# A stack of sequence layers on one core: attention inputs with a swap product, and mixing levels written out with the output scaled once

## The chip, the cores and the metric

The kernel runs on one core of a Trainium2 chip. The metric is the device time of one execution in microseconds (us). Each stage of the kernel ends with a barrier of all engines, so the stages don't overlap. Engines are named as in the profile: PE (matmul; PEld is its weight load), DVE (vector), ACT (scalar), POOL (GpSimd), SP (its queue issues DMAs).

## The reference, cut to what matters

`x` is 2 x 2048 x 256, float32. Eight layers each add their result to `x`: a recurrence, a slot layer, the mixing layer, a slot layer, a long convolution, a ternary layer, attention, a ternary layer. The change touches the mixing layer (`_L0_attn_b`) and the attention (`_L1_attn_b`).

```python
q, v = (qv[..., :c], qv[..., c:])          # qv = x @ attn_W + attn_b
n = 1
while n < t:                                # t = 2048: 11 levels
    prev = concatenate([broadcast(identity, (b, n, c)), q[:, :t - n]], axis=1)
    f = concatenate([prev, q], -1) @ freq_W + freq_b
    z = concatenate([sin(f), cos(f)], -1) @ out_W + out_b
    q = z / (max(abs(z), axis=-1) + 1e-6)
    n *= 2
return (q * v) @ proj_W + proj_b
...
q, k, v = proj(Wq), proj(Wk), proj(Wv)      # 16 heads of 16
re, ro = te * cos - to * sin, te * sin + to * cos    # te, to: even and odd entries of q and of k
```

## The kernel before

**Mixing levels** (`mix_levels_phase`). Between levels the kernel keeps, instead of `q`, the two frequency products of `q` (`parts`, 128 x 2048 for each of two batches). A level has 8 units (`NG`) of 512 tokens (`GT`), 11 levels have 88, in four blocks of 128 tokens (`GP`). For each unit PE sums the two parts, one of them shifted by the level's distance, into `p_f` (`freqs`, L1404 and L1405, four passes). ACT adds the bias (`g`, L1437). DVE takes it into one turn in four operations (L1486 `turns`, L1488 `off`, L1490 and L1492 `red`). POOL clamps it (`arg`, L1472). ACT takes the sine (`sc`, L1441). PE multiplies by the output weights (`products`, L1413, four blocks of 384 columns: 256 of `q` and 128 of the next level's parts). DVE adds the bias (`zb`, L1505, four), takes the largest magnitude of the 256 columns (L1507), adds 1e-6 (L1509) and inverts (`inv`, L1511). ACT multiplies the 128 part columns by `inv` (`scaled`, L1458, four) and the 256 columns of `q` too (`q_out`, L1460, four). PE transposes the scaled parts (`p_t`, L1430) and ACT copies them to `parts` (L1463).

Each engine runs a hardware loop (`Fori`) over the levels with the eight units inside. PE's order in unit m is products(m+1), freqs(m+3), transposes(m); ACT's is sines(m+1), bias(m+2), scaled(m), q_out(m), copy(m); DVE's is zb(m), the maximum, the guard, the reciprocal, and the four operations for unit m+2. Semaphores with counts hand over between engines; the products and frequencies ahead run three units past the last one. `p_z` has one bank for each block, `p_f`, `p_t`, `zb` and the rest have two slots.

**Attention inputs** (`attention_inputs_phase`). 32 units: 8 groups of 512 tokens by 4 blocks of 128 rows of q and k (`UNITS`). PE projects each block twice, with the weights and with the weights of swapped pairs (`c_WqT_pair`, `c_WkT_pair`; L2216, eight passes), and projects 128 tokens of `v` (L2222) from a copy of `xnT` that POOL makes (`xt`, L2200). DVE multiplies by the cosines and the sines (L2235, L2236) and adds (`rot`, L2239). The result is split into three bf16 parts: ACT casts (L2249), POOL subtracts (`rest`, L2202), ACT casts (L2254), POOL subtracts (L2204), SyncE stores the three to DRAM (L2188). All have two slots. The stage `attention_phase` that follows reads them back.

## Time and profile before

| | |
|---|---|
| median of 3 runs | 13537.1 us (13530.22 to 13540.6) |
| the profiled execution | 13516.88 us, span 13515.1 us |
| busy in the span | PE 5932.7, DVE 10018.5, ACT 8441.8, POOL 202.8 us |
| mixing levels | about 10221 to 10804 us of the span |
| attention inputs | about 12042 to 12261 us of the span |

The first four fifths of the span are the recurrence, which the change leaves alone. A row of a timeline gives the start in us, the time in us, the engine, the line, the operation with output and input, how many were merged into the row, and in brackets the idle time before it with what ended it.

### The profile page before, as it was taken

What the parts mean: (1) busy time and instruction counts of PE and PEld (TensorE: products, weight loads), DVE (VectorE), ACT (ScalarE), POOL (GpSimd) and SP (SyncE); (2) the same over time, 40 slices, a digit from 0 to 9 for tenths busy, and PEclk for the clock granted to TensorE, in tenths of its full rate; (3) what the DMA queues carried; (4) which work ended last, traced back from release to release, by engine and by line L of the source; (5) the groups of instructions that cost most, each with busy time, mean ns of one, the idle gap of its engine ahead of it and who ended that gap; (6) DMA issues with size and microseconds to landing.
All of it is one profiled execution on the core that took longest, in us unless ns stands there. A gap on an engine that the chain in (4) does not pass through costs nothing. (4 is left out here: it accounts for less than half of the span.)

```text
span 13515.1 us, 222513 instructions
## 1 busy us (share of the span) xinstructions
PE 5932.7 (44%) x53122; PEld 4394.7 (33%) x53138; DVE 10018.5 (74%) x54576; ACT 8441.8 (62%) x42771; POOL 202.8 (2%) x278
## 2 busy tenths in 40 slices
PE   7222222222222222222222222222267778788998
PEld 6222222222222222222222222222243446653335
DVE  3777777777777777777777777777746838857874
ACT  4666666666666666666666666666635622353665
POOL 0000000000000000000000000000000000011000
PEclk8555555555555555555555555555569978897999
DMA  1100010010001000100010000001000000001100
GB/s 47 20 14 14 15 19 14 14 20 14 14 14 20 14 14 14 20 14 14 14 20 14 14 17 17 14 14 20 14 11 3 2 20 5 7 29 43 29 25 20
DMA packets 339797, 227.46 MB, mean 17 GB/s; under 512 B 27666, under 2 KB 324571, under 8 KB 338272
## 3 DMA queue, kind: packets, MB, share of 16 engines
q1 hardware_dynamic: 338528, 213.76, 7.4%
q8 instruction: 403, 6.60, 0.2%
q14 instruction: 866, 7.09, 0.2%
HBM read 187.87 MB, written 25.43 MB: 16 GB/s over the span
## 5 line engine op out<-in xcount | busy, mean ns | idle before, releaser
L526 PE MATMUL scan_p_car<-scan_hs,scan_mean_mat 32*32 32x2 f32 x16392 | 577.8, 198 | 6838.2 <-DVE scan_hb L653 6825.6
L526 PEld LDWEIGHTS scan_p_car<-scan_hs,scan_mean_mat 32*32 32x32 f32 x16392 | 402.0, 135 | 7017.1 <-DVE scan_hb L653 7004.4
L571 ACT ACTIVATE scan_act_ps<-scan_act_ps 128x64 f32<-128x64 f32 (+1 forms) x8193 | 1642.2, 200 | 64.5
L571 ACT ACTIVATE scan_act_ps<-scan_r 128x64 f32<-128x64 f32 x2048 | 466.2, 228 | 1875.0 <-DVE scan_r L650 1875.0
L553 PE MATMUL scan_p_y<-scan_c_masked,scan_hb 128*64 128x4 f32 x16384 | 1234.2, 253 | 0.0
L531 PE MATMUL scan_p_car<-scan_eps_row,ones 1*128 1x3 f32 x4102 | 1198.3, 360 | 38.7 <-DMA scan_a_log<-L_attn_a_A_log 38.5
L571 ACT ACTIVATE scan_cm<-scan_dl,scan_s 128x64 f32<-128x64 f32 x2049 | 712.2, 348 | 729.0 <-DVE scan_s L676 729.0
L650 DVE TENSOR_TENSOR scan_c<-scan_V,scan_cm 128x64 f32<-128x64 f32 x4096 | 739.4, 222 | 468.8 <-ACT scan_cm L571 423.8
L553 PEld LDWEIGHTS scan_p_y<-scan_c_masked,scan_hb 128*64 128x64 f32 x16384 | 1055.4, 216 | 34.3
L531 PEld LDWEIGHTS scan_p_car<-scan_eps_row,ones 1*128 1x128 f32 x4102 | 1020.6, 308 | 71.4 <-DMA scan_a_log<-L_attn_a_A_log 38.9
L653 DVE SCALAR_TENSOR_TENSOR scan_uw<-scan_w,scan_rsq 128x64 f32<-128x64 f32 x2048 | 461.7, 225 | 659.7 <-ACT scan_rsq L571 654.2
L653 DVE SCALAR_TENSOR_TENSOR scan_products<-scan_p_car,scan_tab 128x2 f32<-128x2 f32 x2049 | 326.4, 159 | 732.8 <-ACT scan_act_ps L571 728.5
L658 DVE TENSOR_SCALAR scan_bx<-scan_step_in,scan_tab 128x64 f32<-128x64 f32 x4098 | 839.6, 247 | 21.9 <-DMA scan_step_in<-scan_scratch 17.4
L653 DVE SCALAR_TENSOR_TENSOR scan_hb<-scan_R,scan_uw 128x64 f32<-128x64 f32 x4096 | 761.6, 223 | 20.9
L2547 ACT ACTIVATE attn_pT<-attn_ps 128x1024 f32<-128x1024 f32 (+3 forms) x640 | 550.2, 896 | 279.9 <-PE attn_ps L2465 168.5
L650 DVE TENSOR_TENSOR scan_w<-scan_c,scan_bx 128x64 f32<-128x64 f32 x4096 | 722.6, 217 | 0.0
L650 DVE TENSOR_TENSOR scan_sq<-scan_w 128x64 f32<-128x64 f32 x4096 | 721.5, 217 | 0.0
L571 ACT ACTIVATE scan_alpha<-scan_step_in,scan_a_neg 128x64 f32<-128x64 f32 x2048 | 681.8, 333 | 18.8 <-issue 18.8
L650 DVE TENSOR_TENSOR scan_V<-scan_hb,scan_F 128x128 f32<-128x128 f32 x2049 | 581.0, 284 | 0.0
L571 ACT ACTIVATE scan_th<-scan_R 128x64 f32<-128x64 f32 x2048 | 524.3, 256 | 65.5
L571 ACT ACTIVATE scan_ru<-scan_act_ps 128x64 f32<-128x64 f32 x2049 | 545.5, 266 | 0.0
L571 ACT ACTIVATE scan_lm<-scan_mag 128x64 f32<-128x64 f32 x2049 | 544.5, 266 | 0.0
(451 smaller groups left out, 17952.2 us busy)
## 6 DMA issues: line engine op xcount, KB each, us to landing
scan_step_in<-scan_scratch SPq DMA_DIRECT2D x520, 256.0 KB, 6.1
qk_scratch<-qkv_parts SPq DMA_DIRECT2D x32, 384.0 KB, 2.5
attn_qT<-qk_scratch SPq DMA_DIRECT2D x192, 64.0 KB, 2.2
attn_kT<-qk_scratch SPq DMA_DIRECT2D x192, 64.0 KB, 2.2
scan_scratch<-prep_dts SPq DMA_DIRECT2D x32, 256.0 KB, 2.1
x<-L_attn_a_x SPq DMA_DIRECT2D x1, 4096.0 KB
out<-x SPq DMA_DIRECT2D x1, 4096.0 KB
filter_taps<-c_kT SPq DMA_DIRECT2D x1, 2048.0 KB
```

The costliest lines, as they stand in the source:

```text
L526: last = nc.tensor.matmul(p_car[slot][rows, 0:2], mean_mat[rows, :], hs[rows, :], start=False, stop=True)
L531: nc.tensor.matmul(p_car[slot][:, 0:3], env["ones"][0:1, :], eps_row[:, :], start=start, stop=not start)
L553: last = nc.tensor.matmul(p_y[par][J * half:J * half + J, k * 4:k * 4 + 4], hb[:, slot, 2 - comp, :], c_masked[:, par, k, comp, 4 * half:4 ...
L571: nc.scalar.activation(dst, src, func, **kw).then_inc(counts[par]["act"], 1)
L650: nc.vector.tensor_tensor(out, a, b, op).then_inc(sem, 1)
L653: nc.vector.scalar_tensor_tensor(out, in0, scalar, in1, op0, op1, **kw).then_inc(sem, 1)
L658: nc.vector.tensor_scalar(bx[:, comp, :], step_in[:, par, k, 1, :], tab[:, par, k, comp:comp + 1], None, ALU.mult).then_inc(sem, 1)
L2547: nc.scalar.activation(pT[(2 * n + pair) % 4][:, :, off:], ps[:, 2 * pair:2 * pair + 2, off:], ACT.Exp).then_inc(exp_done, 1)
```

## The change

In both functions the hardware loops are written out, so that every wait has a constant, and each wait is placed where a slot is reused.

Mixing levels: only the last level writes `q_out`, and only the other ten scale, transpose and copy the parts. PE's order becomes freqs(m+3), products(m+1), transposes(m). ACT reads `p_f` twice, once for `g` and once scaled by 1/(2 pi) for `in_turns`. DVE rounds `in_turns` in one operation (`whole`) and subtracts the two pieces of 2 pi in two; these three for unit m+2 are placed between the steps of the maximum of unit m. Nothing runs past the last unit.

Attention inputs: the swapped weights go. The projection is made once; DVE multiplies it by the sines (`crossed`, with the sign moved to the other entry) and by the cosines (`upright`), PE swaps the pairs of `crossed` by a product with the 128 x 128 permutation `c_swap`, and DVE adds. PE reads `xnT` for `v` without a copy, and ACT copies two blocks of `v` at a time. The two subtractions move from POOL to DVE, which works on four units at once (step m: crossed(m), upright(m), rest(m-2), the last part of m-3, rot(m-1)). `p_w`, `rot` and `rest` have three slots, the bf16 parts four.

The diff, with slot bookkeeping and most removed lines left out:

```diff
 def mix_levels_phase(nc, env):
...
-        turns, off, red, arg, sc = (ph.sb(n, [P, 2, GT]) for n in ("turns", "off", "red", "arg", "sc"))
+        turn_bias = ph.sb("turn_bias", [P, 1])
+        g, in_turns, whole, red, arg, sc = (ph.sb(n, [P, 2, GT]) for n in ("g", "in_turns", "whole", "red", "arg", "sc"))
...
+                def freqs(m):
...
+                    if m >= 2:
+                        pe.wait_ge(g_done, m - 1)
+                        pe.wait_ge(turns_done, m - 1)
+                    if level:
+                        pe.wait_ge(parts_done, m - NG + 1)
+                    nc.tensor.matmul(p_f[m % 2][:, :], sel[:, 0, :], flat[:, at - (1 << level):at - (1 << level) + GT], start=True, stop=False)
+                    nc.tensor.matmul(p_f[m % 2][:, :], sel[:, 1, :], flat[:, at:at + GT], start=False, stop=True).then_inc(f_done, 1)
...
+                def products(m):
...
                     pe.wait_ge(sc_done, m + 1)
                     for k in range(GP):
...
+                        if m:
+                            pe.wait_ge(zb_done, (m - 1) * GP + k + 1)
+                        nc.tensor.matmul(p_z[k][:, 0:W], sc[:, m % 2, k * P:(k + 1) * P], mix[:, :], start=True, stop=True).then_inc(z_done, 1)
...
+                for m in range(M):
+                    if m + 3 < M:
+                        freqs(m + 3)
+                    if m + 1 < M:
+                        products(m + 1)
+                    if m < M - NG:
+                        pe.wait_ge(scaled_done, (m + 1) * GP)
+                        if m >= 2:
+                            pe.wait_ge(parts_done, m - 1)
                         for k in range(GP):
...
+                            last = nc.tensor.transpose(p_t[m % 2][:, k * P:(k + 1) * P], scaled[:, m % 2, k, :], env["ident"][:, :])
                         last.then_inc(t_done, 1)
...
+                def angles(m):
                     act.wait_ge(f_done, m + 1)
...
+                    if m >= 2:
+                        act.wait_ge(high_done, m - 1)
+                    nc.scalar.activation(g[:, m % 2, :], p_f[m % 2][:, :], ACT.Identity, bias=env["freq_bias"][:, 0:1]).then_inc(g_done, 1)
+                    if m >= 2:
+                        act.wait_ge(whole_done, m - 1)
+                    nc.scalar.activation(in_turns[:, m % 2, :], p_f[m % 2][:, :], ACT.Identity, scale=1.0 / (2.0 * np.pi), bias=turn_bias[:, 0:1]).then_inc(turns_done, 1)
+                def sines(m):
...
                     act.wait_ge(arg_done, m + 1)
...
+                    if m >= 2:
+                        act.wait_ge(z_done, (m - 1) * GP)
+                    nc.scalar.activation(sc[:, m % 2, :], arg[:, m % 2, :], ACT.Sin).then_inc(sc_done, 1)
...
+                for m in range(M):
+                    level, b, i = place(m)
+                    if m + 1 < M:
+                        sines(m + 1)
+                    if m + 3 < M:
+                        angles(m + 3)
+                    act.wait_ge(inv_done, m + 1)
+                    if level < LEVELS - 1:
+                        if m >= 2:
+                            act.wait_ge(t_done, m - 1)
                         for k in range(GP):
...
+                            nc.scalar.activation(scaled[:, m % 2, k, :], zb[:, m % 2, k, D:W], ACT.Copy, scale=inv[:, m % 2, k:k + 1]).then_inc(scaled_done, 1)
+                        act.wait_ge(t_done, m + 1)
+                        nc.scalar.activation(parts[:, (level + 1) % 2, b, LEAD + i * GT:LEAD + (i + 1) * GT], p_t[m % 2][:, :], ACT.Copy).then_inc(parts_done, 1)
+                    else:
                         for k in range(GP):
...
+                            nc.scalar.activation(q_out[:, (b * GB + i) * GP + k, :], zb[:, m % 2, k, 0:D], ACT.Copy, scale=inv[:, m % 2, k:k + 1]).then_inc(q_done, 1)
...
+                for m in range(M):
+                    pool.wait_ge(red_done, m + 1)
+                    if m >= 2:
+                        pool.wait_ge(sc_done, m - 1)
+                    nc.gpsimd.tensor_scalar(arg[:, m % 2, :], red[:, m % 2, :], PI_BELOW, -PI_BELOW, ALU.min, ALU.max).then_inc(arg_done, 1)
...
+                def round_off(m):
...
+                    nc.vector.tensor_scalar(whole[:, m % 2, :], in_turns[:, m % 2, :], ROUND, ROUND, ALU.add, ALU.subtract).then_inc(whole_done, 1)
+                def reduce_high(m):
...
+                    nc.vector.scalar_tensor_tensor(red[:, m % 2, :], whole[:, m % 2, :], -TWO_PI_HI, g[:, m % 2, :], ALU.mult, ALU.add).then_inc(high_done, 1)
+                def reduce_low(m):
...
+                    nc.vector.scalar_tensor_tensor(red[:, m % 2, :], whole[:, m % 2, :], -TWO_PI_LO, red[:, m % 2, :], ALU.mult, ALU.add).then_inc(red_done, 1)
...
+                nc.vector.tensor_scalar(turn_bias[:, :], env["freq_bias"][:, :], 1.0 / (2.0 * np.pi), None, ALU.mult).then_inc(bias_done, 1)
...
+                for m in range(M):
...
+                    for k in range(GP):
+                        dve.wait_ge(z_done, m * GP + k + 1)
...
+                        nc.vector.tensor_tensor(zb[:, s, k, :], p_z[k][:, 0:W], mix_bias[:, :], ALU.add).then_inc(zb_done, 1)
+                    dve.wait_ge(zb_done, (m + 1) * GP)
...
+                    nc.vector.tensor_reduce(out=big[:, s, :], in_=zb[:, s, :, 0:D], axis=AX.X, op=ALU.max, apply_absolute_value=True).then_inc(max_done, 1)
+                    if m + 2 < M:
+                        round_off(m + 2)
+                    dve.wait_ge(max_done, m + 1)
+                    nc.vector.tensor_scalar(big[:, s, :], big[:, s, :], EPS_MAX, None, ALU.add).then_inc(guarded, 1)
+                    if m + 2 < M:
+                        reduce_high(m + 2)
+                    dve.wait_ge(guarded, m + 1)
+                    nc.vector.reciprocal(inv[:, s, :], big[:, s, :]).then_inc(inv_done, 1)
+                    if m + 2 < M:
+                        reduce_low(m + 2)
...
 def attention_inputs_phase(nc, env):
...
+    SLOTS_W, SLOTS_R, SLOTS_P = 3, 3, 4
...
-        names = ["c_WqT", "c_WqT_pair", "c_WkT", "c_WkT_pair", "c_WvT"]
+        names = ["c_WqT", "c_WkT", "c_WvT"]
...
+        swap = ph.sb("swap", [P, P])
...
+        upright, crossed = (ph.sb(n, [P, 2, GT]) for n in ("upright", "crossed"))
+        rot, rest = (ph.sb(n, [P, SLOTS_R, GT]) for n in ("rot", "rest"))
+        parts = ph.stack.enter_context(nc.sbuf_tensor("qkv_parts", [P, SLOTS_P, PARTS, GT], BF16))
+        p_w = [ph.ps(f"p_w{k}", [P, GT]) for k in range(SLOTS_W)]
+        p_s = [ph.ps(f"p_s{k}", [P, GT]) for k in range(2)]
+        p_v = [ph.ps(f"p_v{k}", [P, 2, D]) for k in range(2)]
...
+                sp.dma_start(swap[:, :], ins["c_swap"]).then_inc(loaded, 16)
...
+                def project(m):
...
+                    if m >= SLOTS_W:
+                        pe.wait_ge(crossed_done, m - SLOTS_W + 1)
+                        pe.wait_ge(upright_done, m - SLOTS_W + 1)
+                    for k in range(KD):
+                        last = nc.tensor.matmul(p_w[m % SLOTS_W][:, :], w[u // 2][:, k, u % 2 * P:(u % 2 + 1) * P], xnT[:, k, g * GT:(g + 1) * GT],
+                                                start=(k == 0), stop=(k == KD - 1))
+                    last.then_inc(w_done, 1)
+                project(0)
+                project(1)
+                for m in range(M):
+                    if m + 2 < M:
+                        project(m + 2)
+                    if m % 2 == 0 and m >= 4:
+                        pe.wait_ge(v_copied, m // 2 - 1)
+                    for k in range(KD):
+                        last = nc.tensor.matmul(p_v[m // 2 % 2][:, m % 2, :], xnT[:, k, m * P:(m + 1) * P], w[2][:, k, :], start=(k == 0), stop=(k == KD - 1))
+                    if m % 2:
                         last.then_inc(v_done, 1)
+                    pe.wait_ge(crossed_done, m + 1)
+                    if m >= 2:
+                        pe.wait_ge(rot_done, m - 1)
+                    nc.tensor.matmul(p_s[m % 2][:, :], swap[:, :], crossed[:, m % 2, :], start=True, stop=True).then_inc(s_done, 1)
...
+                for step in range(M + 3):
...
+                        nc.vector.scalar_tensor_tensor(crossed[:, m % 2, :], p_w[m % SLOTS_W][:, :], scale, sin[:, i * GT:(i + 1) * GT], ALU.mult, ALU.mult).then_inc(crossed_done, 1)
...
+                        nc.vector.scalar_tensor_tensor(upright[:, m % 2, :], p_w[m % SLOTS_W][:, :], scale, cos[:, i * GT:(i + 1) * GT], ALU.mult, ALU.mult).then_inc(upright_done, 1)
+                    m = step - 2
+                    if 0 <= m < M:
+                        dve.wait_ge(high_done, m + 1)
...
+                        nc.vector.tensor_tensor(rest[:, m % SLOTS_R, :], rot[:, m % SLOTS_R, :], parts[:, m % SLOTS_P, 0, :], ALU.subtract).then_inc(rest_done, 1)
+                    m = step - 3
+                    if 0 <= m < M:
+                        dve.wait_ge(mid_done, m + 1)
+                        nc.vector.tensor_tensor(parts[:, m % SLOTS_P, 2, :], rest[:, m % SLOTS_R, :], parts[:, m % SLOTS_P, 1, :], ALU.subtract).then_inc(low_done, 1)
...
+                    if 0 <= m < M:
+                        dve.wait_ge(s_done, m + 1)
+                        dve.wait_ge(upright_done, m + 1)
...
+                        nc.vector.tensor_tensor(rot[:, m % SLOTS_R, :], upright[:, m % 2, :], p_s[m % 2][:, :], ALU.add).then_inc(rot_done, 1)
...
+                for step in range(M + 2):
...
                         act.wait_ge(rot_done, m + 1)
...
+                        if m >= SLOTS_P:
+                            act.wait_ge(stored[m % SLOTS_P], m // SLOTS_P * 16)
+                        nc.scalar.activation(parts[:, m % SLOTS_P, 0, :], rot[:, m % SLOTS_R, :], ACT.Copy).then_inc(high_done, 1)
+                    m = step - 2
+                    if 0 <= m < M:
+                        act.wait_ge(rest_done, m + 1)
+                        nc.scalar.activation(parts[:, m % SLOTS_P, 1, :], rest[:, m % SLOTS_R, :], ACT.Copy).then_inc(mid_done, 1)
+                    if step < M and step % 2:
+                        j = step // 2
+                        act.wait_ge(v_done, j + 1)
+                        nc.scalar.activation(v[:, 2 * j:2 * j + 2, :], p_v[j % 2][:, :, :], ACT.Copy).then_inc(v_copied, 1)
...
-    for w in ("Wq", "Wk"):
-        arrays[f"c_{w}T_pair"] = np.ascontiguousarray(arrays[f"c_{w}T"].reshape(D, D // 2, 2)[:, :, ::-1].reshape(D, D))
+    arrays["c_swap"] = (p[:, None] == (p ^ 1)[None, :]).astype(np.float32)
...
-    arrays["c_sin"] = (np.sin(turn) * np.where(p % 2 == 0, -1.0, 1.0)[:, None]).astype(np.float32)
+    arrays["c_sin"] = (np.sin(turn) * np.where(p % 2 == 0, 1.0, -1.0)[:, None]).astype(np.float32)
```

## Rows read from the trace of the kernel before

**Rows 1.** Timeline (start us, us, engine, line ...) at both ends of the mixing levels

```profile
10236.86 2.74 PE L1413 MATMUL mix_p_z<-mixing_levels_mix,mix_sc 128*128 128x384 f32 x8
...
10237.06 0.69 ACT L1437 ACTIVATE mix_g<-mix_p_f,mixing_levels_freq_bias 128x512 f32<-128x512 f32 x1 [1.94 <-PE mix_p_f L1405]
...
10791.84 2.84 PE L1413 MATMUL mix_p_z<-mixing_levels_mix,mix_sc 128*128 128x384 f32 x8 [1.45 <-ACT mix_sc L1441]
...
10803.48 0.60 ACT L1463 ACTIVATE mixing_levels_parts<-mix_p_t 128x512 f32 x1 [1.99 <-PE mix_p_t L1430]
```

**Rows 2.** Windows: stretch, us; busy PE, PEld, DVE, ACT, POOL; clock, DMA share, GB/s

```profile
10236.00:10800.00 564.00, 437.12 (x1401) 235.86 (x1400) 495.76 (x963) 388.99 (x963) 53.29 (x87) 1.00 0.00 0
...
12100.00:12200.00 100.00, 79.60 (x194) 39.19 (x193) 33.18 (x48) 24.81 (x49) 46.30 (x49) 0.91 0.18 63
...
12500.00:12700.00 200.00, 194.87 (x1309) 69.31 (x1304) 166.35 (x428) 128.90 (x155) 1.04 (x1) 1.00 0.11 30
```

**Rows 3.** The timeline of one mixing unit, ACT

```profile
10487.25 0.60 ACT L1463 ACTIVATE mixing_levels_parts<-mix_p_t 128x512 f32 x1 [2.00 <-PE mix_p_t L1430]
10487.75 0.62 ACT L1441 ACTIVATE mix_sc<-mix_arg 128x512 f32<-128x512 f32 x1
10488.26 0.68 ACT L1437 ACTIVATE mix_g<-mix_p_f,mixing_levels_freq_bias 128x512 f32<-128x512 f32 x1
10488.83 1.27 ACT L1458 ACTIVATE mix_scaled<-mix_zb,mix_inv 128x128 f32<-128x128 f32 x4
10490.00 1.70 ACT L1460 ACTIVATE mixing_q_out<-mix_zb,mix_inv 128x256 f32<-128x256 f32 x4
```

**Rows 4.** The same unit, DVE

```profile
10488.98 0.43 DVE L1486 TENSOR_SCALAR mix_turns<-mix_g 128x512 f32<-128x512 f32 x1 [0.57 <-ACT mix_g L1437]
...
10490.62 0.69 DVE L1492 SCALAR_TENSOR_TENSOR mix_red<-mix_off,mix_red 128x512 f32<-128x512 f32 x1
...
10491.23 1.95 DVE L1505 TENSOR_TENSOR mix_zb<-mix_p_z,mixing_levels_mix_bias 128x384 f32<-128x384 f32 x4
...
10493.21 1.22 DVE L1507 TENSOR_REDUCE mix_big<-mix_zb 128x4 f32<-128x1024 f32 x1
...
10494.47 0.17 DVE L1509 TENSOR_SCALAR mix_big<-mix_big 128x4 f32<-128x4 f32 x1
...
10494.67 0.18 DVE L1511 RECIPROCAL mix_inv<-mix_big 128x4 f32<-128x4 f32 x1
```

**Rows 5.** The same unit, PE and POOL

```profile
10488.50 2.84 PE L1413 MATMUL mix_p_z<-mixing_levels_mix,mix_sc 128*128 128x384 f32 x8 [1.45 <-ACT mix_sc L1441]
...
10491.17 1.02 PE L1404 MATMUL mix_p_f<-mixing_levels_parts,mix_sel 128*128 x2
...
10492.89 0.60 PE L1430 MATMUL mix_p_t<-ident,mix_scaled 128*128 128x128 f32 x4
...
10491.50 0.61 POOL L1472 TENSOR_SCALAR mix_arg<-mix_red 128x512 f32<-128x512 f32 x1 [5.83 <-DVE mix_red L1492]
```

**Rows 6.** The timeline within the attention inputs

```profile
12153.50 0.82 DVE L2239 TENSOR_TENSOR qkv_rot<-qkv_t 128x512 f32<-128x512 f32 x1
...
12154.63 1.13 PE L2222 MATMUL qkv_p_v<-qkv_w,qkv_xt 128*128 128x256 f32 x4 [2.49 <-POOL qkv_xt L2200]
...
12155.59 3.60 PE L2216 MATMUL qkv_p_w<-xnT,qkv_w 128*128 x8
...
12159.03 1.03 PE L2222 MATMUL qkv_p_v<-qkv_w,qkv_xt 128*128 128x256 f32 x4
```

**Rows 7.** The timeline at both ends of the attention inputs

```profile
12041.62 0.38 SPq L2177 DMA_DIRECT2D qkv_w<-c_WqT  x1
...
12054.12 5.29 PE L2216 MATMUL qkv_p_w<-xnT,qkv_w 128*128 x8 [14.34 <-DMA qkv_sin<-c_sin]
...
12256.73 1.15 POOL L2204 TENSOR_TENSOR qkv_parts<-qkv_rest,qkv_parts 128x512 bf16<-128x512 f32 x1 [0.76 <-ACT qkv_parts L2254]
...
12261.50 0.84 SPq L2370 DMA_DIRECT2D attn_o_sum<-c_causal  x2
```

## Prediction before the run

> **What bounds the kernel now.** I read the timeline first for the borders of the two stages that are edited, then the busy time by stretch, then one unit of each stage engine by engine. Every stage ends in a barrier, so what a stage saves is saved whole. The chain that ended last on the page covers only the last stages and says nothing here.
>
> The mixing levels run 88 units. From the start of `products(1)` to that of `products(87)` are 86 intervals, 10236.86 to 10791.84 us, 6.453 us each [rows 1]. In that stretch PE is busy 437 of 564 us, DVE 496, ACT 389, POOL 53, and PE is granted its full clock, 2.4 GHz [rows 2]. No engine is full, so a cycle between engines sets the pace. One unit shows it: PE starts the products at 10488.50, then runs the frequency sums and the transposes [rows 5]; ACT copies a unit's transposes out from 10487.25, and only then, at 10487.75, takes the sines that PE's products wait for [rows 3]; a unit later, at 10493.70, the copy comes 0.20 after the transposes' end at 10493.49. The cycle is products 2.67 (10488.50 to 10491.17), sums 1.72 (to 10492.89), transposes 0.60, about 0.20 to the copy, copy 0.50 to the sines, sines 0.62, 0.13 to PE: 6.44, the interval measured (0.01 off). PE idles 1.45 of it, waiting for the sines [rows 5].
>
> The attention inputs run 32 units from 12054.12 to 12257.88, where POOL ends (6.37 a unit), and the next stage's SyncE issues at 12261.50 [rows 7]: 207.4 us. Here POOL is busiest per unit of work (46 of 100 us) yet PE has 80 and a clock of 0.91 [rows 2]. Every second unit PE waits 2.49 us for POOL's copy of `xnT`, which stands on POOL behind two subtractions, which wait for ACT's casts, which wait for DVE's rotation [rows 6]. So this too is a cycle, through four engines.
>
> **Mixing levels, part by part.** `q_out` is now scaled in the last level alone: 80 x 4 ACT instructions go (1.70 us a unit [rows 3]). They lay beside ACT's wait for the transposes and are worth nothing themselves; they leave room for what is added. Added on ACT is `in_turns`, a second reading of `p_f` like the `g` reading: 0.57 from start to start (10488.26 to 10488.83 [rows 3]). ACT per unit becomes copy 0.50, sines 0.51, two readings 1.14, `scaled` 1.17: 3.3 us. In the last level it is 0.51 + 1.14 + 1.60 = 3.3.
>
> DVE loses one 0.43 operation a unit (round, unround and scale become one), and the reduction of unit m+2 is dealt out between the steps of the maximum. A step that waits for the one before it starts 0.04 after its end (10493.21 + 1.22 to 10494.47); one that doesn't starts 0.08 before it (10490.62 + 0.69 to 10491.23) [rows 4]. Sum: `zb` to the maximum 1.98, maximum 1.14 net of the overlap, `round_off` 0.35, guard 0.09, `reduce_high` 0.61, reciprocal 0.10, `reduce_low` 0.61: 4.88 us. Its extra waits (turns, high, whole, slots) are for results of a unit before, and cost nothing while that holds.
>
> PE keeps its work: 2.67 + 1.72 + 0.60 less the 0.15 overlap = 4.84 us. What changes is the order: `freqs(m+3)` now stands ahead of `products(m+1)`, so while ACT copies the transposes and takes the sines (0.20 + 0.50 + 0.62 + 0.13 = 1.45), PE has 1.72 of sums. The old cycle is covered, with 0.27 to spare. What is late next is the cycle sums, readings, `scaled`, transposes: freqs end to `g` 0.20 (10236.86 to 10237.06 [rows 1]), 0.57, 0.57, `scaled` 1.27, 0.13 to PE, transposes 0.45, the next sums 1.72: 4.91. `scaled(m)` also needs `inv(m)`: the last `zb` starts 0.2 after the products end, and `inv` follows 0.55 + 0.03 + 1.14 + 0.35 + 0.09 + 0.61 + 0.18 = 2.95 later, thus 3.15 after the products; with the transposes behind them (0.45), sums (1.72) and two readings (1.34 with the hand-over) ACT comes there after 3.51. It is covered by 0.36. Behind ACT's wait for `inv` stand `scaled`, the copy and the sines; they are in the cycles counted. POOL's clamp (0.61 [rows 5]) ends before ACT wants it. Three limits, 4.84, 4.88 and 4.91, lie within 0.07 of each other and will disturb one another a little; I take 4.95.
>
> In the last level there are no transposes, so PE needs 4.39, ACT 3.3, DVE 4.88; 4.88 holds. Saved: 79 intervals x (6.45 - 4.95) = 118.5, and 7 x (6.45 - 4.88) = 11.0. The end: before, 12.2 us pass from `products(87)` to the end of the last copy (10791.84 to 10804.08 [rows 1]), for a unit beyond the last is begun too. After: 2.67 + 0.2 + 0.55 + 0.03 + 1.22 + 0.04 + 0.17 + 0.03 + 0.18 + 0.07 + 1.70 = 6.9. That is 5.3 more, 134.8 us in all. The start gains `freqs(2)` before `products(0)` and one tiny `turn_bias`, and loses `freqs(3)` behind; I take nothing, -1 to +2 us.
>
> The levels are written out, which removes register work and the branch. Across ten turns of the loop the mean interval is 6.453 where one unit takes 6.45, so branches cost nothing that shows. The Trainium skill (Runtime: NRT & Kernel Launch, Instruction fetch mechanics) says that a taken branch may stall the fetch and that written-out code streams; this trace shows no such stall, so by the rule the gain would be larger and by the row it is zero. I take the row.
>
> **Attention inputs, part by part.** Instead of the two projections of a unit (eight passes of PE) there is one (four), and one swap product of 128 by 512 (two). Eight passes take 3.44 (12155.59 to 12159.03), the `v` product 1.03 less 0.16 overlap = 0.87 [rows 6]. PE per unit: projection 1.72, `v` 0.87, swap (one fp32 product of 512 columns, a quarter of 3.44) 0.86: 3.45 us. POOL's copy and both its subtractions go; DVE takes the subtractions: five operations of 0.69 with 0.08 overlap (the bound from the rows of DVE [rows 4]), 3.05; with no overlap at all 3.5. The subtractions read `bf16`; no DVE row of this stage shows that, and I bound it by POOL's 1.15 above and 0.61 below, taking 0.61 since DVE's rotation, with the same length and two SBUF operands, takes 0.69 when undisturbed; it was stretched to 0.82 beside POOL's copy [rows 6], which also goes. ACT: two casts of 0.53 and half a `v` copy, 1.4. PE is the limit if the waits are hidden: the swap of m waits for `crossed(m)`, whose projection ended two units earlier; behind it on PE stands `project(m+3)`, whose slots were read two steps before. DVE's `rot(m-1)` waits for a swap that is a step old and is DVE's last of the step; behind it stands `crossed(m+1)`, with a unit of slack. ACT's cast waits for a store four units back, 13.8 us; from POOL's end to the next stage the store, its landing and the barrier took 3.6 [rows 7]. The stores' share of the DMA goes from 0.18 at 6.37 us a unit to 0.33 [rows 2], far from full. I take 3.45.
>
> Sum: start about 1.0 earlier (two of five weights of 256 KB go and 64 KB of `c_swap` come, 0.45 of the 3.3 MB whose loading fills the 12.5 us from 12041.62 to 12054.12; 0 to 1.7 [rows 7]), 32 x 3.45 = 110.4, the first passes at 1.2 GHz (5.29 against 3.60 for eight) +1.7, then rotation, casts and subtractions of the last unit 0.2 + 0.69 + 0.1 + 0.63 + 0.07 + 0.69 + 0.1 + 0.63 + 0.1 + 0.69 = 3.9, and 3.6 to the next stage: 12053.1 + 119.6 = 12172.7, against 12261.5. Saved 88.8.
>
> **Total.** 134.8 + 88.8 = 223.6 us. The profiled execution took 13516.9, its span 13515.1; it would take 13293.3. The median of the runs is 20.2 above it; 13537.1 - 223.6 = 13313.5.
>
> **The rivals.**
> A, DVE's order buys nothing: then the three hand-overs dealt out keep their 0.12 each and DVE needs 5.24, 86 x 0.3 = 26 us less gain, about 13339. The Trainium skill (VectorE: DVE Perf Modes, The DRAIN you can't avoid) states it so: the next operation can't start until the pipe is empty, waits or none. In this trace operations without a wait between them overlap by 0.08 [rows 4], against the rule. With a further coupling of the three near-equal limits the interval could reach 5.4, 13352. Chance 0.16.
> B, the attention inputs run at 4.0 us, for DVE with its bf16 operands at 0.8 each: 17 us less, 13331; with subtractions at POOL's 1.15, 4.13 a unit, 13335. Chance 0.08.
> C, one part only pays, for its new waits close another cycle: 13402 if only the mixing does, 13448 if only the inputs do. Every wait named reaches back a unit or more, against it. Chance 0.04.
> D, slower: PE is granted 1.2 GHz in both stages. Passes then take double: 4.84 becomes 9.7 against 6.45 and 3.45 becomes 6.9 against 6.37, +281 and +17 less the 5 at the end, near 13830. It decides from a mean granted clock under about 0.69, where 87 x 4.84 + 32 x 3.45 over the clock reaches the present 765 us. Against: at 195 of 200 us busy PE keeps 1.00 here, and the 0.91 of the inputs stands behind PE's own pauses [rows 2, 6]. Chance 0.02.
> E, the parts do not act and nothing moves: 13537. The busy sums forbid it. Chance 0.02.
> Forecast 0.68.
>
> Range: 13285 (all limits at their lower values, 5 us at the start, and 0.1% between measurements) to 13372 (A and B together, with the same). It leaves out C to E. 0.2% is 27 us, about what a measurement can tell from no change. Faster 0.96, same 0.02, slower 0.02.
>
> **What would show it.** The mixing levels' interval near 4.95 with PE, DVE idle under 0.2 each and ACT waiting for `inv` or transposes; `q_out` 32 times, not 352; the inputs' interval at 3.45 with PE never waiting over 0.2, POOL idle, clock 1.0 in both. PE waiting for the sines again, or DVE busy all of a longer interval, would prove the cycles misread.

## The result, and the profile after

The changed kernel takes 13301.3 us (median of 3 runs, 13299.2 to 13316.4) against 13537.1 before: a ratio of 0.983, 95% interval 0.981 to 0.985, 235.8 us less. The forecast was 223.6 less. The profiled execution took 13299.2 us, its span 13297.4, 217.7 under the span before. The two edited stages together saved 227.4; totals scatter by some us around that, and the stages are the firmer number.

| us, in the profiled execution | before | after | saved | forecast |
|---|---|---|---|---|
| mixing levels, first sums to the next stage's first DMA | 581.5 | 440.3 | 141.2 | 134.8 |
| attention inputs, first load to the next stage's first DMA | 219.9 | 133.7 | 86.2 | 88.8 |
| all other stages | 12713.7 | 12723.4 | -9.7 | 0 |

Busy time by stretch, after, in the middle of both stages (stretch, length; busy PE, PEld, DVE, ACT, POOL with counts; granted clock of PE, DMA share, GB/s):

```profile
10241.00:10633.00 392.00, 391.87 (x1278) 206.63 (x1277) 389.02 (x800) 283.08 (x638) 48.60 (x80) 1.00 0.00 1
11930.00:12030.00 100.00, 100.00 (x294) 55.48 (x292) 89.40 (x145) 42.18 (x73) 0.00 (x0) 1.00 0.32 111
```

Beside [rows 2], PE's idle time is gone in both. In the mixing levels DVE has next to none left either (389.02 of 392). The inputs run at the full clock, 1.00 where it was 0.91. One mixing unit, after, on PE, DVE and ACT in turn:

```profile
10488.66 2.74 PE L1419 MATMUL mix_p_z<-mixing_levels_mix,mix_sc 128*128 128x384 f32 x8
10491.35 0.66 PE L1435 MATMUL mix_p_t<-ident,mix_scaled 128*128 128x128 f32 x4
10491.84 1.02 PE L1410 MATMUL mix_p_f<-mixing_levels_parts,mix_sel 128*128 128x512 f32 x2
...
10490.54 1.94 DVE L1524 TENSOR_TENSOR mix_zb<-mix_p_z,mixing_levels_mix_bias 128x384 f32<-128x384 f32 x4
10492.52 1.22 DVE L1528 TENSOR_REDUCE mix_big<-mix_zb 128x4 f32<-128x1024 f32 x1
10493.66 0.42 DVE L1496 TENSOR_SCALAR mix_whole<-mix_in_turns 128x512 f32<-128x512 f32 x1
10493.99 0.16 DVE L1532 TENSOR_SCALAR mix_big<-mix_big 128x4 f32<-128x4 f32 x1
10494.11 0.69 DVE L1503 SCALAR_TENSOR_TENSOR mix_red<-mix_whole,mix_g 128x512 f32<-128x512 f32 x1
10494.72 0.17 DVE L1536 RECIPROCAL mix_inv<-mix_big 128x4 f32<-128x4 f32 x1
10494.83 0.69 DVE L1508 SCALAR_TENSOR_TENSOR mix_red<-mix_whole,mix_red 128x512 f32<-128x512 f32 x1
...
10487.14 0.60 ACT L1476 ACTIVATE mixing_levels_parts<-mix_p_t 128x512 f32<-128x512 f32 x1 [0.75 <-PE mix_p_t L1435]
10487.64 0.62 ACT L1455 ACTIVATE mix_sc<-mix_arg 128x512 f32<-128x512 f32 x1
10488.86 0.69 ACT L1445 ACTIVATE mix_g<-mix_p_f,mixing_levels_freq_bias 128x512 f32<-128x512 f32 x1 [0.60 <-PE mix_p_f L1411]
10489.45 0.68 ACT L1448 ACTIVATE mix_in_turns<-mix_p_f,mix_turn_bias 128x512 f32<-128x512 f32 x1
10490.02 1.28 ACT L1474 ACTIVATE mix_scaled<-mix_zb,mix_inv 128x128 f32<-128x128 f32 x4
```

PE's 1.45 us before the products [rows 5] is no longer there: the sums fill it. ACT now pauses, 0.75 for the transposes and 0.60 for the sums. The copy and `g` behind these pauses serve later units, but `scaled`, which PE needs in this one, stands behind `g` in ACT's order. DVE's steps from `zb` to `zb` add up to 4.90. So does the cycle through the others: sums 1.72, hand-over to `g` 0.20, `g` 0.59, `in_turns` 0.57, `scaled` 1.33 to the transposes at 10491.35, 0.49 to the next sums, together 4.90. `inv` ends at 10494.89 (10494.72 + 0.17), and the next `scaled`, one unit after the row above, starts at 10494.92: ACT comes to it just as `inv` is there. Nearly every interval between the starts of two maxima is 4.90; the last, behind which nothing is reduced any more, is 3.52, and the mean of all 87 is 4.886.

The attention inputs after, a unit on PE and a part of it on DVE, then two issues of SyncE's queue, the first matmul, the last unit's swap product and rotation, and the next stage's first DMA:

```profile
11971.82 1.88 PE L2233 MATMUL qkv_p_w<-xnT,qkv_w 128*128 128x512 f32 x4
11973.53 1.03 PE L2245 MATMUL qkv_p_v<-qkv_w,xnT 128*128 128x256 f32 x4
11974.40 1.02 PE L2251 MATMUL qkv_p_s<-qkv_crossed,qkv_swap 128*128 128x512 f32 x2
...
11974.42 0.68 DVE L2278 TENSOR_TENSOR qkv_parts<-qkv_rest,qkv_parts 128x512 bf16<-128x512 f32 x1
11975.46 0.69 DVE L2286 TENSOR_TENSOR qkv_rot<-qkv_upright,qkv_p_s 128x512 f32<-128x512 f32 x1 [0.35 <-PE qkv_p_s L2251]
...
11906.55 0.38 SPq L2210 DMA_DIRECT2D qkv_w<-c_WqT  x1
11908.00 1.52 SPq L2211 DMA_DIRECT2D qkv_swap<-c_swap  x1
...
11918.29 7.27 PE L2233 MATMUL qkv_p_w<-xnT,qkv_w 128*128 128x512 f32 x12 [13.57 <-DMA qkv_sin<-c_sin]
...
12029.42 1.02 PE L2251 MATMUL qkv_p_s<-qkv_crossed,qkv_swap 128*128 128x512 f32 x2
...
12032.63 0.68 DVE L2286 TENSOR_TENSOR qkv_rot<-qkv_upright,qkv_p_s 128x512 f32<-128x512 f32 x1
...
12040.27 0.87 SPq L2420 DMA_DIRECT2D attn_o_sum<-c_causal  x2
```

A unit is 1.71 + 0.87 + 0.86 = 3.44 us of PE without a pause, where [rows 6] had eight passes and a wait of 2.49 in every second one.

### The profile page after: what moved, and what is told of

Same layout as the page of the kernel before. It is cut to its first block and busy times, and to the rows that moved or that the text cites. A ratio compares the mean times of both kernels' runs of the same rounds, so it can differ in the third digit from the quotient of the medians.

```text
span 13297.4 us, 219906 instructions
## 1 busy us (share of the span) xinstructions
PE 5863.1 (44%) x53022; PEld 4357.3 (33%) x53022; DVE 9979.3 (75%) x54545; ACT 8357.6 (63%) x42480; POOL 109.4 (1%) x180
```

## The experiments

All kernels that ran, with both stages as each profile shows them. The totals are medians of 3 runs for the first two, 4 for the next two and 5 for the last two; the other eight ran once, so their totals are weak and their stages carry the argument. "Interval" is the mean from one maximum's start to the next, over 87. The kernel before took 13525.9 beside the first eight experiments, 13537.1 beside the next two, 13536.5 beside the last two.

| kernel | total | mixing stage | interval | inputs stage | mixing starts at |
|---|---|---|---|---|---|
| before | 13537.1 | 581.5 | 6.444 | 219.9 | 10223.4 |
| after | 13301.3 | 440.3 | 4.886 | 133.7 | 10231.5 |
| e_mix_only | 13383.6 | 440.1 | 4.886 | 221.9 | 10227.9 |
| e_inputs_only | 13444.6 | 581.7 | 6.444 | 132.9 | 10231.9 |
| e_pe_order | 13466.6 | 523.0 | 5.799 | 220.3 | 10231.2 |
| e_no_interleave | 13334.2 | 475.7 | 5.294 | 134.0 | 10231.2 |
| e_less_dve | 13289.8 | 435.8 | 4.837 | 133.9 | 10226.7 |
| e_less_act | 13294.4 | 439.8 | 4.886 | 136.0 | 10226.7 |
| e_less_both | 13278.8 | 423.3 | 4.699 | 133.6 | 10231.2 |
| e_q_each_level | 13301.0 | 452.6 | 5.025 | 134.1 | 10222.5 |
| e_pool_subtracts | 13293.1 | 440.1 | 4.886 | 133.4 | 10225.7 |
| e_two_projections | 13315.9 | 440.2 | 4.886 | 158.8 | 10227.0 |
| e_pool_rounds | 13316.0 | 448.7 | 4.931 | 133.0 | 10238.1 |
| e_after_again | 13305.3 | 440.0 | 4.886 | 133.9 | 10234.4 |

The last column matters for reading the others. All work ahead of the mixing levels is the same in all fourteen, and still they start 15.6 us apart. In the two kernels before and after, 6.5 of the 8.1 us between their starts arise in a routing stage near 9970 us, where PE is granted a mean clock of 0.73 and 0.88 of full speed in two 15 us stretches before and of 0.61 in both after. In `e_after_again` it is another stretch: 10.8 of its 11.1 us against the kernel before build up bit by bit along the recurrence. So totals of two kernels differ by some us for reasons that aren't theirs; the stage columns, where they stand apart, carry what follows.

**Each part alone.** Edit one: the new `mix_levels_phase` in the kernel before. Edit two: all of the change but that function.

```diff
 e_mix_only:     before + def mix_levels_phase of after
 e_inputs_only:  after  + def mix_levels_phase of before
```

> The kernel before with the new mixing levels alone. My theory: the two stages are separate (a barrier between every two stages), so this gives the mixing's share whole: first sum of frequencies to the next stage's first DMA 440 us against 581, some 141 us less than before, ratio about 0.9896. Rival (one change frees or costs something in the other, or in the stages between): a saving that, with that of the inputs alone, does not add up to that of both within 12 us.

> The kernel before with the new attention inputs alone. My theory: 86 us less than before (133.7 us from the stage's first DMA to the next stage's, against 219.9), ratio about 0.9936; the mixing levels stay at 6.45 us a unit. Rival: not additive, or the shorter stage makes the attention that follows slower by several us.

Measured: ratios 0.989 (0.988 to 0.991) and 0.994 (0.992 to 0.996), 142.3 and 81.3 us less. They add to 223.7. That is 12.1 short of the 235.8 of both, just outside the 12 that was named, but 7.5 short of the 231.2 of `e_after_again`, and the totals come from different sets of runs. The stages decide it: each new stage keeps its length within 1 us whether the other is new or old (440.1 and 440.3, 132.9 and 133.7), and what follows the attention inputs takes 1253 to 1258 us with old inputs and with new. Rival C falls.

**PE's order alone**, in the kernel before:

```diff
-                        products(j + 1, m + 1)
                         ahead = j + 3
                         freqs(level + ahead // NG, ahead % NG, m + 3)
+                        products(j + 1, m + 1)
```

> The kernel before with one edit in the mixing levels: PE runs freqs(m+3) ahead of products(m+1). My theory: the old cycle (products, sums, transposes, copy, sines: 6.44) opens, as 1.72 us of sums now cover the copy and the sines, and DVE takes over: its four operations behind the maximum give 1.98 + 1.26 + 0.20 + 0.20 + 0.46 + 0.46 + 0.72 + 0.61 = 5.9 us a unit, some 47 us of the 141. Rival 1: the writing out of the loops is what pays; then it stays at 6.44. Rival 2: the order alone brings the whole gain; then 4.9.

Measured: 5.80 an interval, the stage 58.5 us shorter. DVE in one unit, then ACT:

```profile
10485.66 1.94 DVE L1505 TENSOR_TENSOR mix_zb<-mix_p_z,mixing_levels_mix_bias 128x384 f32<-128x384 f32 x4
10487.63 1.22 DVE L1507 TENSOR_REDUCE mix_big<-mix_zb 128x4 f32<-128x1024 f32 x1
...
10489.19 0.43 DVE L1486 TENSOR_SCALAR mix_turns<-mix_g 128x512 f32<-128x512 f32 x1
...
10491.45 1.94 DVE L1505 TENSOR_TENSOR mix_zb<-mix_p_z,mixing_levels_mix_bias 128x384 f32<-128x384 f32 x4
...
10489.31 1.28 ACT L1458 ACTIVATE mix_scaled<-mix_zb,mix_inv 128x128 f32<-128x128 f32 x4 [1.35 <-DVE mix_inv L1511]
```

DVE goes from one unit to the next without a pause in 5.79, and ACT waits 1.35 for its `inv`. The swap of two blocks on PE broke the old cycle, and DVE's own work was next. It also speaks on the loop: this kernel keeps it, one unit takes 5.79 and the mean over ten turns of it is 5.80, so the branches cost nothing that shows here. In the kernel before, where DVE has slack, one interval in eight, once a turn of the loop, is 6.52 where the others are 6.44 to 6.47, some 0.07 us a turn; whether that is the branch or the step to the next level was not parted. The Trainium skill (Runtime: NRT & Kernel Launch, Instruction fetch mechanics) lets one expect a stall at a taken branch whose target is not yet fetched; neither trace shows a larger one than that 0.07.

**DVE's three reductions behind the reciprocal**, in the changed kernel:

```diff
-                    if m + 2 < M:
-                        round_off(m + 2)
                     dve.wait_ge(max_done, m + 1)
...
                     nc.vector.reciprocal(inv[:, s, :], big[:, s, :]).then_inc(inv_done, 1)
                     if m + 2 < M:
+                        round_off(m + 2)
+                        reduce_high(m + 2)
                         reduce_low(m + 2)
```

> The changed kernel with the three reductions of unit m+2 all behind the reciprocal, not dealt out between the steps of the maximum. My theory: each dependent step costs 0.04 after the end before it in place of 0.08 before it, six hand-overs in place of three, and DVE goes from 4.90 to about 5.26 us a unit, some 30 us more in all. Rival (the order buys nothing, each operation waits for an empty pipe whatever stands between): 4.90, no change.

```profile
10486.61 1.22 DVE L1528 TENSOR_REDUCE mix_big<-mix_zb 128x4 f32<-128x1024 f32 x1
10487.86 0.17 DVE L1530 TENSOR_SCALAR mix_big<-mix_big 128x4 f32<-128x4 f32 x1
...
10488.16 0.42 DVE L1496 TENSOR_SCALAR mix_whole<-mix_in_turns 128x512 f32<-128x512 f32 x1
10488.61 0.69 DVE L1503 SCALAR_TENSOR_TENSOR mix_red<-mix_whole,mix_g 128x512 f32<-128x512 f32 x1
10489.34 0.69 DVE L1508 SCALAR_TENSOR_TENSOR mix_red<-mix_whole,mix_red 128x512 f32<-128x512 f32 x1
...
10491.92 1.22 DVE L1528 TENSOR_REDUCE mix_big<-mix_zb 128x4 f32<-128x1024 f32 x1
```

The same operations take 5.31 instead of 4.90 and the stage 35.4 us more. Where one waits for the one before it, it starts 0.03 or 0.04 behind its end (10486.61 + 1.22 to 10487.86; 10488.61 + 0.69 to 10489.34); the dealt-out ones start 0.08 ahead of it (10494.11 + 0.69 to 10494.72 above). Rival A falls: the order alone is worth 0.41 us a unit. With this the 1.55 us that the interval lost are all named: 0.65 by PE's order, 0.48 between this kernel's 5.31 and the 5.79 above, about the one operation of 0.46 from start to start that DVE lost, and 0.41 here. That leaves some 0.02 for the written-out loops, which had no run of their own. The Trainium skill (VectorE: DVE Perf Modes, The DRAIN you can't avoid) says that chaining without semaphores saves nothing; the 5.31 and 4.90 speak against it. The same section adds that an operation that isn't held starts earlier, and with that the traces agree.

**Which limit sets 4.90.** One leaves out `reduce_low`, the small part of the reduction; one leaves out `in_turns`, so DVE rounds `g` itself and the division by 2 pi is missing; one leaves out both. None gives the reference's angles in full.

```diff
 e_less_dve:   -  nc.vector.scalar_tensor_tensor(red, whole, -TWO_PI_LO, red, mult, add)
 e_less_act:   -  nc.scalar.activation(in_turns, p_f[m % 2], Identity, scale=1.0 / (2.0 * np.pi), bias=turn_bias)
 e_less_both:  -  both
```

> The changed kernel without reduce_low (the small piece of 2 pi is not subtracted), so 0.61 us less on DVE a unit. My theory: in the changed kernel two limits tie at 4.90, DVE (no idle) and the cycle sums, two readings, scaled, transposes (0.20 + 0.59 + 0.57 + 1.33 + 0.49 + 1.72 = 4.90); so with DVE at 4.29 the interval stays at 4.90 (4.86 to 4.90). Rival (DVE alone sets the pace): PE's own 4.78.

> The changed kernel without the second reading of p_f: DVE rounds g itself, so the division by 2 pi is left out, and ACT has 0.57 us less a unit; DVE keeps its operations. My theory: the cycle falls to 4.33 but DVE holds the interval at 4.90. Rival (the cycle alone sets the pace): PE's 4.78.

> The changed kernel without reduce_low and without the second reading of p_f (the small piece of 2 pi and the division by 2 pi left out). My theory: both of the tied limits are gone, the third stays: PE at 2.57 + 0.49 + 1.72 = 4.78 us a unit, PE never idle. Rival: something else holds 4.90 (for one the copy and the sines, which have 0.27 to spare).

Measured, in the levels with transposes: 4.89 a unit without `reduce_low`, 4.90 without `in_turns`, and 4.73 without both. PE's sums in the first, where DVE has 0.61 less to do, and a whole unit of PE in the last, which never pauses:

```profile
10486.13 1.02 PE L1410 MATMUL mix_p_f<-mixing_levels_parts,mix_sel 128*128 128x512 f32 x2
10491.01 1.02 PE L1410 MATMUL mix_p_f<-mixing_levels_parts,mix_sel 128*128 128x512 f32 x2
...
10486.80 0.60 PE L1434 MATMUL mix_p_t<-ident,mix_scaled 128*128 128x128 f32 x4
10487.24 1.02 PE L1409 MATMUL mix_p_f<-mixing_levels_parts,mix_sel 128*128 128x512 f32 x2
10488.10 1.02 PE L1410 MATMUL mix_p_f<-mixing_levels_parts,mix_sel 128*128 128x512 f32 x2
10488.95 2.74 PE L1418 MATMUL mix_p_z<-mixing_levels_mix,mix_sc 128*128 128x384 f32 x8
10491.53 0.60 PE L1434 MATMUL mix_p_t<-ident,mix_scaled 128*128 128x128 f32 x4
```

So DVE's work is a limit of 4.90 and the cycle through ACT one of 4.89, each enough by itself, and PE's own is 4.73: transposes 0.44, sums 1.71, products 2.58. Its columns give the same: a unit streams 8 x 384 + 4 x 512 + 4 x 128 = 5632, and two passes of 512 take 0.86, so an estimate from that row is 4.73. In the kernels with 4.89 and 4.90 the products take 2.67 to 2.69 and the transposes 0.49. PE is "busy" 391.87 of 392 us in the changed kernel and yet isn't the limit: short waits between its groups are counted as busy. The last level has no transposes and so no such cycle. There DVE alone holds 4.90 in the changed kernel, and without `reduce_low` the interval is 4.30; that is most of the 4.5 us by which this kernel's stage is shorter (4.837 is its mean over all units).

**`q_out` in every level again**, in the changed kernel:

```diff
+                    for k in range(GP):
+                        nc.scalar.activation(q_out[...], zb[:, m % 2, k, 0:D], ACT.Copy, scale=inv[...]).then_inc(q_done, 1)
                     if level < LEVELS - 1:
```

> The changed kernel with q_out scaled in all eleven levels as before. My theory: ACT's sum goes from 3.34 to 0.50 + 0.51 + 0.59 + 0.57 + 1.17 + 1.61 = 4.95 and ACT, never idle, sets 4.95 to 5.0 us a unit: 4 to 8 us more in all. Rival 1 (the instructions lie beside waits, worth nothing): 4.90. Rival 2 (the copy of the parts comes 0.85 later behind them and pushes the sines and the products): 5.4 or more, 40 us.

Measured: interval 5.025, stage 12.3 us longer, above the 4 to 8 expected (the total hides it, since this one starts the stage 9 us earlier). ACT over one unit, then PE's next products:

```profile
10487.80 0.69 ACT L1445 ACTIVATE mix_g<-mix_p_f,mixing_levels_freq_bias 128x512 f32<-128x512 f32 x1 [0.17 <-PE mix_p_f L1411]
...
10491.72 0.58 ACT L1479 ACTIVATE mixing_levels_parts<-mix_p_t 128x512 f32<-128x512 f32 x1
10492.20 0.62 ACT L1455 ACTIVATE mix_sc<-mix_arg 128x512 f32<-128x512 f32 x1
10492.72 0.69 ACT L1445 ACTIVATE mix_g<-mix_p_f,mixing_levels_freq_bias 128x512 f32<-128x512 f32 x1
...
10492.88 0.91 PE L1419 MATMUL mix_p_z<-mixing_levels_mix,mix_sc 128*128 128x384 f32 x2 [0.19 <-ACT mix_sc L1455]
```

ACT's own work is 4.92 (`g` to `g`, without a pause), a third limit beside the other two. But the units alternate between 4.92 and 5.19. After a unit in which ACT never pauses its sines come late and PE waits 0.19 for them; then PE's sums come late and ACT waits 0.17 for those, as in the first row. Between 10300 and 10600 us each of these waits stands 30 times, in every second unit. The mean of the two is 5.05, 0.13 over the largest limit.

**The inputs' parts.** The subtractions on POOL again, in the new order; and a second projection in place of the swap product (its weights are not swapped, so the rotation is another one):

```diff
 e_pool_subtracts:
-                        nc.vector.tensor_tensor(rest[...], rot[...], parts[..., 0, :], ALU.subtract)
+                        nc.gpsimd.tensor_tensor(rest[...], rot[...], parts[..., 0, :], ALU.subtract)
 e_two_projections:
-                    nc.tensor.matmul(p_s[m % 2], swap, crossed[:, m % 2, :], start=True, stop=True)
+                    for k in range(KD):
+                        nc.tensor.matmul(p_s[m % 2], w[u // 2][:, k, ...], xnT[:, k, ...], start=(k == 0), stop=(k == KD - 1))
```

> The changed kernel with the attention inputs' two subtractions on POOL instead of DVE, in the new order (step m: rest(m), then the last part of m-1). My theory: what held the old stage was the chain through POOL's copy, not where the subtractions run; POOL needs 2.3 us a unit, DVE 1.8, PE 3.44, so the interval stays at 3.44 and only the end grows by about 1 us. DVE's rotation may stretch beside POOL (0.69 to 0.95 before). Rival (POOL's latency in the chain casts, subtractions, slots closes a cycle): 4 us a unit or more, 18 us.

> The changed kernel with a whole second projection (four passes) in place of the swap product (two passes), so the result lacks the swap. My theory: PE is the limit of the stage and the interval goes from 3.44 to 1.72 + 0.87 + 1.72 = 4.30, 27 us more for the stage. Rival (DVE or a hand-over holds 3.44 and PE has room): less than 4.1.

With the subtractions on POOL, at 1.16 each, the stage is 133.4 against 133.7 with them on DVE, the same (it is 132.9 to 136.0 in the kernels that leave it alone). With two projections PE's unit is 4.29 and the stage 25.1 us longer:

```profile
11970.20 1.88 PE L2233 MATMUL qkv_p_w<-xnT,qkv_w 128*128 128x512 f32 x4
11971.91 1.03 PE L2245 MATMUL qkv_p_v<-qkv_w,xnT 128*128 128x256 f32 x4
11972.78 1.88 PE L2253 MATMUL qkv_p_s<-xnT,qkv_w 128*128 128x512 f32 x4
11974.49 1.88 PE L2233 MATMUL qkv_p_w<-xnT,qkv_w 128*128 128x512 f32 x4
```

Of the 86 us that the inputs gain, the swap product is thus worth 25, in the new order. The other 61 come with all else that changed there: the order that lets PE run on, the `xnT` copy that is gone, the added slots, the loops written out. These were not parted, so that the copy held the old stage is read from the rows and not shown by a run. Where the subtractions are made is worth nothing in the new order.

**A try at a faster one: the rounding on POOL**, against the changed kernel once more.

```diff
+                    nc.gpsimd.tensor_scalar(in_turns, g, 1.0 / (2.0 * np.pi), ROUND, ALU.mult, ALU.add)
+                    nc.gpsimd.tensor_scalar(whole, in_turns, ROUND, None, ALU.subtract)
-                    nc.scalar.activation(in_turns, p_f[m % 2], Identity, scale=1.0 / (2.0 * np.pi), bias=turn_bias)
-                    nc.vector.tensor_scalar(whole, in_turns, ROUND, ROUND, ALU.add, ALU.subtract)
```

> The changed kernel with the rounding on GpSimd (g/2pi plus the rounding constant, then minus the constant: two of its tensor_scalar of 0.61 us beside the clamp, 1.84 of a unit) instead of one reading on ScalarE and one operation on VectorE. It asks whether what the kernels with work left out gained can be had with all of the work done. VectorE would then need 1.98 + 1.25 + 0.12 + 0.61 + 0.11 + 0.61 = 4.68 us a unit, the cycle sums, reading, scaled, transposes about 4.3, PE alone 4.73 (its unit in the kernel with both left out). Theory: 4.73, so 79 x 0.17 = 13 us less than the changed kernel in the mixing stage, 427, and near 13287 in all. Rival: the maximum, then its reciprocal, come at a place in the unit where scaled and the transposes stay late, and PE goes on at 4.90, stage 440, nothing gained. Second rival: GpSimd beside VectorE stretches VectorE's operations (0.69 to over 0.75, as the rotation was stretched to 0.82 beside the copy before), VectorE takes over 4.9 and the stage is longer than 440.

> The changed kernel once more, as it is, to compare the kernel with the rounding on GpSimd on the same chip. Expected: 13301 us within 10, mixing stage 440.3, interval 4.90, inputs stage 133.7 within 2; what differs from the first profile lies ahead of the mixing levels, where the work is the same in all kernels (their start spread from 10222.5 to 10231.9 us over the kernels run).

Measured: the stage takes 448.7, 8.7 us longer than the 440.0 of `e_after_again`, not 13 shorter, and the total is 13316.0 beside 13305.3. POOL, then DVE:

```profile
10487.80 0.78 POOL L1483 TENSOR_SCALAR mix_in_turns<-mix_g 128x512 f32<-128x512 f32 x1 [1.69 <-ACT mix_g L1444]
10488.66 1.80 POOL L1487 TENSOR_SCALAR mix_whole<-mix_in_turns 128x512 f32<-128x512 f32 x1
10490.43 0.61 POOL L1496 TENSOR_SCALAR mix_arg<-mix_red 128x512 f32<-128x512 f32 x1
...
10487.41 0.69 DVE L1505 SCALAR_TENSOR_TENSOR mix_red<-mix_whole,mix_g 128x512 f32<-128x512 f32 x1
10488.13 0.98 DVE L1510 SCALAR_TENSOR_TENSOR mix_red<-mix_whole,mix_red 128x512 f32<-128x512 f32 x1
```

The second rival came true. `reduce_low`, 0.69 alone, takes 0.98 while POOL ends its first operation and begins its second, and DVE's unit is 4.94. The Trainium skill (SBUF — State Buffer, SBUF: two separate sides) has DVE operations with two SBUF inputs and POOL operations that read SBUF exclude each other. The stretching agrees with that in kind, but not in size: `reduce_low` overlaps POOL's first operation by 0.45 and POOL's first overlaps `reduce_high` by 0.30, so a whole block would give 1.14 and, at the clamp's 0.61, 0.91, where the rows have 0.98 and 0.78. The 1.80 doesn't follow from it either: 0.45 of overlap with `reduce_low` and 0.61 make 1.06. Why this form, one subtraction of a constant, takes so long on POOL stays open.

## Why the prediction was right, point by point

- **The old cycle of the mixing levels** was read rightly: with PE's order alone it was gone, and the levels went from 6.45 to 5.80, not further, since DVE then needed 5.79. That the loop's turn costs nothing that shows was read from a mean; unit by unit the kernel before has about 0.07 us a turn, under 1 us in all.
- **The interval** was forecast at 4.95 and is 4.90. The three limits were put at 4.84, 4.88 and 4.91. The last two are 4.90 and 4.89. The first is 4.73: the 2.67 for the products in [rows 5] was taken for work, but PE was idle just before them, and such a group's row is 2.84 where one that follows without a pause is 2.74 [rows 1]; 0.09 of it was start. The 0.04 added for mutual disturbance was mis-sized by all of itself. With two limits close together there was none that shows, since DVE's own steps give the 4.90; with a third at 4.92, in the kernel with `q_out` in each level, there was 0.13. The room of 0.36 that `inv` was to have before `scaled` was 0.03: DVE, never idle, came later to `zb` than the sum has it. It cost nothing. The term of 129.5 us came out as 134.6 (86 intervals of 6.453 less 420.4).
- **The two ends**: from `products(87)` to the end of the last copy 7.2 us against a forecast of 6.9, 5.1 us saved for 5.3. From the first sums to `products(1)` 11.9 for 13.5 before, 1.6 us gained where nothing was taken.
- **`q_out`** "worth nothing itself" was right for the kernel before, and "leaves room" has a size now: 12.3 us once the rest is fast.
- **DVE's order**, the largest doubt (rival A), is worth 35 us, by the overlap of 0.08 that [rows 4] had shown.
- **The attention inputs**: 3.44 a unit for 3.45. The subtractions with bf16 operands take 0.68 to 0.69 on DVE, 0.61 from start to start, as forecast, and DVE has room: it waits 0.35 a unit for the swap product.
- **The inputs' start and end** were put too short, so that the stage saved 2.6 less than forecast. The first matmul stands 11.7 us behind the first load, not 12.5: 0.8 gained, not 1.0. That is luck in part: the same stretch is 10.4 to 12.9 us over the eleven kernels with the new inputs and 12.5 to 13.4 over the three with the old. The issue of `c_swap` held SyncE's queue 1.52 us here, but 0.47 in most others; eight of the fourteen profiles have one issue of 1.37 to 1.76, mostly another load's. The first passes, at a granted clock of 0.50 in their first 4 us, cost 1.9 more than at full clock and not 1.7. The last unit's end was mis-sized most: 5.8 us pass from its swap product (over at 12029.42 + 0.86 = 12030.28) to DVE's end at 12036.08, not 3.9, since in DVE's fixed order two subtractions of earlier units, one with a wait for ACT, stand ahead of `rot(31)`, at 12032.63. And 4.2 instead of 3.6 pass from there to the next stage. The slightly shorter unit gives 0.3 back.
- **Outside both stages** the profiled execution after was 9.7 us slower, 8.1 of it ahead of the mixing levels. That point has a spread of 15.6 over fourteen kernels whose work is the same up to there, so this says nothing of the change. The two medians differ by 235.8, the stages by 227.4; the 8 between them is of that same size. That the total came out 12.2 below the forecast 13313.5 is thus luck for two thirds; the stages account for 3.8.
- **Rival B** did not happen, nor **D**: the clock was 1.00 in the middle of both stages, and nor **E**.

## What to carry to other kernels

Where no engine is full, write the cycle of hand-overs out from one unit's rows until it meets the measured interval. Then an edit of the order alone can be priced: the next interval is the largest of what is left, each engine's own sum and each remaining cycle. Before counting on an operation that leaves one of these limits, list all that stand within some per cent of it; here taking away either of two gained 0.01 us a unit or nothing, both together 0.17. And put independent operations between dependent ones on DVE: here it cost nothing and was worth 0.41 us of a unit of 5.31.

## What the runs showed of the hardware

- On DVE a dependent operation started 0.03 to 0.04 us behind the end of the one before it, an independent one 0.08 ahead of it. Three such places dealt out took 0.41 us from a unit of 5.31.
- On POOL a `tensor_scalar` of 128x512 took 0.61 us as a clamp, 0.78 with a multiply and an add, and 1.80 with one subtraction (medians of 88, the latter two beside DVE). DVE's 0.69 beside them became 0.98.
- PE counted as busy 391.87 of 392 us at 4.90 a unit, while its own work, seen in another kernel, is 4.73.
- A point of time ahead of the change came up to 15.6 us apart between kernels; in the one pair that was taken apart, most of the difference stood where PE's granted clock differed.
- In eight of fourteen profiles one load's issue on SyncE's queue in the attention inputs, not always the same one, took 1.37 to 1.76 us where the others took 0.38 to 0.54.
- With three limits within 0.03 us of each other (4.89 to 4.92) units alternated between 4.92 and 5.19.
